# Last chunk's gather of a soft mixture-of-experts dispatch written to other PSUM banks, the first second-layer block placed after it, and loops of two chunks in place of four

## What is computed

```python
xn = layernorm(x, gamma, beta)                       # 16 experts, 16 slots, hidden 32
logits = einsum('bnd,des->bnes', unit(xn) * scale, unit(mu))
dispatch = softmax(logits, axis=1)                   # over the 64 positions
combine = softmax(logits over all 256 experts and slots)
slot_in = einsum('bnd,bnes->besd', xn, dispatch)
h = gelu(einsum('besd,edh->besh', slot_in, w1) + b1)
slot_out = einsum('besh,ehd->besd', h, w2) + b2
out = einsum('besd,bnes->bnd', slot_out, combine)    # added to x
```

## Time and profile before

| | us |
|---|---|
| median of three runs | 531.99 |
| the profiled execution, its own time | 533.24 |
| its span in the trace | 531.3 |
| PE busy in the span | 480.1 (90%) |
| DVE busy | 400.3 (75%) |
| ACT busy | 366.3 (69%) |
| POOL busy | 291.8 (55%) |

### The profile page before, as it was taken

The page is one execution under the profiler, slowest core; times in us unless marked ns, Lnnn a source line. Parts: engine busy times, 40 slices in busy tenths (PEclk is TensorE's granted clock), DMA queues, the critical chain, the costliest instruction groups (busy, mean ns, idle before and its releaser), DMA issues. The chain is left out here.

```text
span 531.3 us, 21606 instructions
## 1 busy us (share of the span) xinstructions
PE 480.1 (90%) x8732; PEld 326.2 (61%) x8732; DVE 400.3 (75%) x1095; ACT 366.3 (69%) x554; POOL 291.8 (55%) x398
## 2 busy tenths in 40 slices
PE   3999968989779999999998789999999996998995
PEld 2777746655346666666665556565656565777884
DVE  4778668889998898989978666565766534777895
ACT  3888735655678788887878488878787655654550
POOL 4434233555677778687848665898898712011000
PEclk9999999999999999999999999999999997999999
DMA  5377448540001101010111011223232324355554
GB/s 188 84 176 199 133 128 199 148 122 0 3 24 26 44 25 46 25 45 25 30 41 45 1 80 63 104 84 103 84 104 83 105 83 141 121 166 169 175 183 116
DMA packets 53322, 49.46 MB, mean 93 GB/s; under 512 B 14064, under 2 KB 40944, under 8 KB 53232
## 3 DMA queue, kind: packets, MB, share of 16 engines
q1 hardware_dynamic: 53232, 48.20, 30.5%
HBM read 30.87 MB, written 17.04 MB: 90 GB/s over the span
## 5 line engine op out<-in xcount | busy, mean ns | idle before, releaser
L612 DVE TENSOR_REDUCE c_mx<-ps 128x16 f32<-128x1024 f32 x64 | 77.9, 1218 | 12.2 <-PE ps L794 12.1
L552 POOL TENSOR_TENSOR copies_or_layer<-k_or_hidden,w_mask 128x512 bf16<-128x512 f32 x80 | 83.6, 1070 | 1.2 <-DVE c_work L643 1.2
L713 ACT ACTIVATE c_work<-ps 128x2048 f32<-128x2048 f32 x32 | 59.9, 1873 | 26.9 <-PE ps L823 26.9
L1471 ACT ACTIVATE copies_or_layer<-k_or_hidden 32x512 f32<-32x512 f32 (+1 forms) x64 | 40.2, 628 | 28.7 <-PE ps L1499 28.0
L1484 DVE TENSOR_TENSOR o_slot_out<-ps,w_b 128x512 f32<-128x512 f32 x64 | 41.1, 684 | 8.9 <-PE ps L1499 8.2
L1348 ACT ACTIVATE e_slot_in<-ps 128x1024 f32<-128x1024 f32 x30 | 30.6, 1020 | 24.7 <-PE ps L1399 24.7
L1302 POOL TENSOR_TENSOR e_scaled<-e_raw,e_rden 128x512 f32<-128x512 f32 x16 | 20.8, 1301 | 46.1 <-DMA e_rden<-dispatch_inverses 46.1
L1499 PE MATMUL ps<-w_w,copies_or_layer 64*32 64x128 f32 x2048 | 40.6, 283 | 3.3 <-issue 3.2
L723 ACT ACTIVATE c_q_bd<-x_all,w_mask 128x512 f32<-128x512 f32 x64 | 42.7, 715 | 0.0
L1399 PE MATMUL ps<-copies_or_layer,v_or_front 64*128 64x256 f32 x256 | 37.2, 410 | 4.3 <-DVE e_raw L1328 2.7
L1576 PE MATMUL ps<-o_slot_out,ctx_sb 128*64 128x129 f32 x512 | 37.5, 282 | 1.7 <-issue 1.4
(11 more groups left out here) (166 smaller groups left out, 1182.8 us busy)
## 6 DMA issues: line engine op xcount, KB each, us to landing
x_all<-x_scratch SPq DMA_DIRECT2D x64, 128.0 KB, 2.9
combine_scratch<-v_or_front SPq DMA_DIRECT2D x16, 512.0 KB, 2.8
ctx_sb<-combine_scratch SPq DMA_DIRECT2D x16, 512.0 KB, 3.5
x_sb<-in_x SPq DMA_DIRECT2D x16, 256.0 KB, 3.3
x_scratch<-a_x SPq DMA_DIRECT2D x16, 256.0 KB, 2.5
ctx_sb<-in_ctx SPq DMA_DIRECT2D x16, 256.0 KB, 3.0
e_rden<-dispatch_inverses SPq DMA_DIRECT2D x64, 64.0 KB, 2.0
out<-o_y SPq DMA_DIRECT2D x32, 128.0 KB, 3.1
```

The costliest lines, as they stand in the source:

```text
L552: ins = nc.gpsimd.tensor_tensor(k_bd[:, c.m2, s, :], k32[:, c.v, :], w["mask8"][:, s:s + 1].to_broadcast([P, TOK]), ALU.mult)
L612: nc.vector.reduce_max(mx[:, c.m2, :, p], ps[:, SCORE:SCORE + 2, :].rearrange("p a (h m) -> p (a h) m", m=N), AX_X).then_inc(mx_sb.sem, 1)
L713: nc.scalar.activation(prob[:, h, :], ps[:, 0:4, :].rearrange("p a b -> p (a b)"), ACT.Exp, scale=float(HD) ** -0.5).then_inc(p_sb.sem, 1)
L1471: ins = self.nc.scalar.activation(self.h_bd[at, c.m2, :, :, e % 2, :].rearrange("p s g k -> p g s k"), self.hidden[at, :, bass.ts(c.v, SC ...
```

## The change

Three things are done.

1. The gather of the last chunk (15) goes to banks 3 and 4 (first half) and 1 and 2 (second half) instead of 6 and 7. Both halves wait for `disp_sb` and `comb_sb` of chunk 15 and no longer for `raw_sb` of chunk 14 or for the copy of the first half. DVE's slot copies read those banks. The wait for `raw_sb` of chunk 14 moves to the first layer of chunk 15.
2. `layer` of chunk 0 of the second stage comes after the first layer and the sums of chunk 15 instead of before them.
3. The second stage's loops have bodies of two chunks. On PE and ACT they cover chunks 2 to 13 in six rounds, on DVE and SP 4 to 13 in five rounds; before it was 4 to 11 in two rounds of four on all. The semaphores of the `comb` loads and of the output DMAs are pairs instead of fours.

```diff
-    def __init__(self, i, k):
-        self.i, self.k = i, k
+    def __init__(self, i, k, n=4):
+        self.i, self.k, self.n = i, k, n
...
-        self.v = k if i is None else i * 4 + k
+        self.v = k if i is None else i * n + k
...
+        self.half = k // 2 if i is None else i * (n // 2) + k // 2
...
-def walk(eng, step, first, last, lo, hi):
+def walk(eng, step, first, last, lo, hi, n=4):
...
-    with eng.Fori(0, (hi - lo) // 4) as i:
-        for r in range(4):
-            step(Chunk(i, lo + r))
+    with eng.Fori(0, (hi - lo) // n) as i:
+        for r in range(n):
+            step(Chunk(i, lo + r, n))
...
                             nc.vector.tensor_copy(slot_in[:, c.m2, 4 * h:4 * h + 4].rearrange("p (a r) e -> p r a e", r=2),
-                                                  ps[:, 6:8, :].rearrange("p r (a e) -> p r a e", a=2)).then_inc(in_sb.sem, 1)
+                                                  ps[:, (3, 1)[h]:(5, 3)[h], :].rearrange("p r (a e) -> p r a e", a=2)).then_inc(in_sb.sem, 1)
...
                 pe.wait_ge(disp_sb.sem, disp_sb.at(c))
-                if h:
+                bank = 6 if c.plus(1) else (3, 1)[h]
+                if not c.plus(1):
+                    pe.wait_ge(comb_sb.sem, comb_sb.at(c))
+                elif h:
                     pe.wait_ge(in_sb.sem, in_sb.at(c, 1))
...
-                        ins = nc.tensor.matmul(ps[:, 6 + r, a * ES:(a + 1) * ES], xn[at, c.m4, 2 * h + a, :],
+                        ins = nc.tensor.matmul(ps[:, bank + r, a * ES:(a + 1) * ES], xn[at, c.m4, 2 * h + a, :],
...
-                if t.k == CHUNKS - 1:
-                    pe.wait_ge(disp_sb.sem, disp_sb.at(end))
-                    pe.wait_ge(comb_sb.sem, comb_sb.at(end))
-                    for u in range(2):
-                        layer.layer(pe, Chunk(None, 0), u)
                 c = t.plus(0)
                 if c:
                     pe.wait_ge(in_sb.sem, in_sb.at(c))
+                    if not c.plus(1): pe.wait_ge(raw_sb.sem, raw_sb.at(c.plus(-1)))
...
                     ins.then_inc(den_ps.sem, 1)
+            for u in range(2):
+                layer.layer(pe, Chunk(None, 0), u)
...
-        self.comb_in = kit.landings("o_comb_in")
+        self.comb_in = kit.pairs("o_comb_in")
...
-        y_out = kit.landings("o_y_out", 2)
+        y_out = kit.pairs("o_y_out", 2)
...
-        last, hi = CHUNKS, CHUNKS - 4
+        last, hi = CHUNKS, CHUNKS - 2
...
-            walk(sp, step, 0, last, 4, hi)
+            walk(sp, step, 0, last, 4, hi, 2)
...
-            walk(act, step, 0, last, 4, hi)
+            walk(act, step, 0, last, 2, hi, 2)
...
-            walk(dve, step, 0, last, 4, hi)
+            walk(dve, step, 0, last, 4, hi, 2)
...
-            walk(pe, step, 0, last, 4, hi)
+            walk(pe, step, 0, last, 2, hi, 2)
```

More of the change, by code:

```diff
@@ L37, in plus @@
             return None
-        return Chunk(self.i, self.k + j)
+        return Chunk(self.i, self.k + j, self.n)
 class Signal:
@@ L73, in at @@
     def at(self, c):
-        return (c.v // 2 + 1) * (16 * self.per)
-def walk(eng, step, first, last, lo, hi):
-    hi = lo + (hi - lo) // 4 * 4
+        return (c.half + 1) * (16 * self.per)
+def walk(eng, step, first, last, lo, hi, n=4):
+    hi = lo + (hi - lo) // n * n
     for t in range(first, lo):
         step(Chunk(None, t))
-    with eng.Fori(0, (hi - lo) // 4) as i:
-        for r in range(4):
-            step(Chunk(i, lo + r))
+    with eng.Fori(0, (hi - lo) // n) as i:
+        for r in range(n):
+            step(Chunk(i, lo + r, n))
     for t in range(hi, last):
@@ L1523, in step @@
                     dispatch.tail_sp(sp, t.k)
-            walk(sp, step, 0, last, 4, hi)
-            for k in range(CHUNKS - 4, CHUNKS):
+            walk(sp, step, 0, last, 4, hi, 2)
+            for k in range(CHUNKS - 2, CHUNKS):
                 sp.wait_ge(y_out.of(Chunk(None, k)), y_out.at(Chunk(None, k)))
```

## The result

The changed kernel takes 528.89 us (median of 4 runs, 527.87 to 530.01) against 532.17 us of the kernel before (median of 4): ratio 0.9929, 95% interval 0.9906 to 0.9952, so 2.6 to 5.0 us faster. The forecast was 529.0. The total was met, but the two terms behind it were not: the experiments give the loops nearly three times what I gave them (5.2 and 5.4 us against 1.8), and the seam nothing that can be measured. The profiled execution took 530.01 us.

The account below looks back on a forecast made before the run. From 455.37 us PE alone was taken as the bound, waiting for its own first-run instructions. Seam 1.2 + loops 2.0 - branches 0.2 = 3.0 us off 531.99 gave a median of 529.0 us, range 527.2 to 531.6.

Parts of the forecast that it names:

- the seam: Stretch between dispatch and second layer, up to `combine(0, 1)`; the moved gather and layer were to gain 1.2 us there (0.6 to 3.3).
- Part 1: Gather of chunk 15: both halves back to back, 439.6 to 441.8 us, 1.1 us each, beside DVE's copy of `e_raw`.
- the signs: Marks of being right: gathers end by 442, `combine(0, 1)` at 454 to 454.4, issue waits 2.3 to 2.9 us, rounds 8.70 to 8.75.
- Part 2 and what is late next: Second layer of chunk 0 ends by 448.3 us; then DVE's unmoved inversion of chunk 14, 452.56, holds `combine(0, 1)` until 453.95.
- I take 1.2 us: Gain chosen for `combine(0, 1)` starting earlier, between 1.1 us if the clock falls and 1.4 otherwise; ends 0.6 and 3.3.
- The gaps up to step 3: PE's waits for instructions before step 4 of the second layer: 0.69, 0.34 and 0.73 us, claimed to stay.
- Part 3: Two-chunk loops: first-run steps on PE fall from 12 to 6, saving 2.0 us (0.5 to 3.0), less 0.2 for branches.
- 1.95 us: PE's gaps in steps 4 to 7, 0.17 + 1.46 + 0.32, claimed saved because that code has already run.
- The 0.2 us for branches: Cost of four more taken branches on PE, 0.05 us each, set against the gain from the loops.
- the second rival: Stretch before `combine(0, 1)` gives all of its 3.3 us, sums of chunk 14 landing earlier: 526.9 us; chance 0.05.
- The rival of fetching at every branch: Each branch back on PE fetches code anew at 1.46 us: 4.6 us slower, 536.6; chance 0.09, shared with other such waits.
- The rival of one part alone: Only the stretch before `combine(0, 1)` or only the loops pays: 0 to 2.2 us gained, 529.8 to 532; chance 0.22.

Follow-up runs that it names:

- the seam alone: Gather of chunk 15 into other banks and second layer of chunk 0 moved, loops of four kept, against the kernel before: 0.9991, again 1.0017.
- the written-out kernel: Changed kernel with all 16 second-layer steps written out on every engine, no loop or branch: 1.0051 of the kernel before.
- short loads: Kernel before, with comb loads from chunk 2 on cut to 64 fp32 a partition: 0.9934; with the changed gather and layer order too, 0.9924.

## Why the prediction was right, and where its steps were not

**Part 1** went as worked out: the half gathers back to back from 0.39 us after the sums on, 2.00 us for both, no cost at the moved wait. The absolute times of the signs do not fit (the gathers end at 442.90, not by 442, and `combine(0, 1)` starts at 455.07), because S lies at 440.51 us in this profile and at 439.14 in that of before.

**Part 2 and what is late next** were right locally. The inversion of chunk 14 stayed where the memory's way puts it, 12 us behind the one before, and `combine(0, 1)` came right behind two shifts. The seam became 1.4 to 2.1 us shorter in the changed kernel (14.56 and 14.13 against 16.23 and 15.93), over my 1.2. But the step "I take 1.2 us" stood as a gain of the whole kernel. Parts 1 and 2 alone measured 0.5 us under before in one run and 0.9 us over it in the other, each with no change inside its interval; a gain of 1.2 us lies inside the first interval and outside the second. I had treated the stretch after 455.37 us as PE's alone and did not follow DVE's next wait on memory: the inversion of chunk 15 cost PE 2.04 us in one profile of the changed kernel and 0.32 in the other, and behind the first wait the clock fell in both, some 1.3 us each time, which I had put only ahead of it. In the profiles of the seam alone the first wait stands too, but neither the fall of the clock nor the second wait; there it is the code gaps that are longer. The gaps up to step 3, which I had staying (0.69, 0.34, 0.73), did not stay either: the changed kernel has 0.38 and 0.21 there in one profile, 0.43, 0.62 and 0.35 in the other, so PE's issue waits sum to 1.0 and 1.4 us, not to 2.3 to 2.9.

**Part 3** was the mis-sized term: 2.0 less 0.2 us forecast, 5.2 and 5.4 measured (3.5 to 7.3 over both runs' intervals). The step that failed is "1.95 us" for the gaps of steps 4 to 7: idle time read as price. The round took 20.43 us, where four chunks without a gap take 17.4 (4 x 4.35). The last column of the table, 0.06 forecast and 1.3 measured, has the same fault and one more: the gap of 0.50 us that was to stay went too. These two places hold 4.5 us. The 0.2 us for branches was too high: rounds of 8.69 and 8.71 us are two chunks of 4.35. DVE with register addresses did not become the bound.

Two figures of the working are loose, and the forecast rests on neither: the 452.1 us of part 2 is not worked out from the 450.9 before it, and "1.0 + 4.1" of the second rival is 3.3 for the seam and 1.8 for the loops, split another way.

**The sum** was right by luck: the seam's 1.2 us did not come, and the loops gave more than that above their 1.8. The single ratios (0.9929 and 0.9905, 3.8 and 5.1 us) do not tell how much of the seam is in it.

**The rival of fetching at every branch** fell: no packet of queue 8 between 472 and 492 us, in which PE branches back three times, and written-out code is the slow form. The Trainium skill, page Runtime: NRT & Kernel Launch, section Instruction fetch mechanics, counts the crossing of a 16 KiB boundary as mostly hidden, and by its rule on taken branches this change would be slower. The runs disagree with both: a new packet went with 0.5 to 0.65 us of the kernel's time, and a branch back with nothing measurable. **The rival of one part alone** was in substance what happened, with the loops as that part and at nearly three times their price.

**Open:** what sets the length of a code gap (the loads of `comb` do not in the kernel before, and may with the seam), why it was longer in the seam-only runs and in the written-out kernel (steps 4 to 7: 22.1, 23.4 and 21.6 us) but not with short loads (20.1), where the rest of the short loads' 3.5 us lies, which of the two inversions gives how much (neither was tried alone), and whether the seam is worth anything within the changed kernel.

## What to carry to other kernels

Price a gap in PE's stream by the time from group to group against one without a gap, not by the idle that the trace shows. Where PE issues some 320 matmuls and weight loads a chunk, new code is a cost of its own: leave as few steps as possible to be run for the first time. Here six such steps in place of twelve gave some 1%; six in place of eight could not be told apart. Before moving work ahead of a wait, follow each later wait on memory of the engine it feeds; the transfer keeps its own time, and here moving two small reciprocals behind the work that PE needs went with 2.6 to 3.9 us, where the seam alone gave nothing measurable.

## What the runs showed of the hardware

In the changed kernel a loop body of two chunks, about 40 KB by its packets (five of 16 KB came for four chunks of the kernel before), ran six rounds; no packet of queue 8 arrived from 472 to 516 us, and a round took 8.69 or 8.71 us, where two chunks at 4.35 without a branch are 8.70. In the kernel before a body of four, some 80 KB, came round once without one. A packet of 16 KB of new code went with 0.5 to 0.65 us of the kernel's time in three comparisons with 5, 8 and 13 packets (an estimate that puts all of the difference down to the packets; 0.3 to 0.9 with the intervals of the first two). A stop of PE inside a group costs about 0.3 us more than it shows (1.80 for 1.46, 0.60 for 0.32, 0.52 for 0.17).
